# Second attention with one folded query-key product, the normalised image as its keys, and gamma and beta moved into the group norm

## The reference, cut to what matters

```python
def _L1_conv_ref(inputs, gn_gamma, gn_beta, wq, bq, wk, bk, wv, bv, wo, bo):
    GROUPS = 32
    xg = inputs.astype(jnp.float32).reshape(B, H, W, GROUPS, C // GROUPS)
    mean = jnp.mean(xg, axis=(1, 2, 4), keepdims=True)
    var = jnp.var(xg, axis=(1, 2, 4), keepdims=True)
    xg = (xg - mean) * jax.lax.rsqrt(var + EPS)
    x = xg.reshape(B, H, W, C) * gn_gamma + gn_beta
    q = jnp.einsum('bhwc,cd->bhwd', x, wq) + bq
    k = jnp.einsum('bhwc,cd->bhwd', x, wk) + bk
    v = jnp.einsum('bhwc,cd->bhwd', x, wv) + bv
    q = q.reshape(B, N, C) * (1.0 / jnp.sqrt(jnp.float32(C)))
    scores = jnp.einsum('bnc,bmc->bnm', q, k.reshape(B, N, C))
    attn = jax.nn.softmax(scores.astype(jnp.float32), axis=-1)
    out = jnp.einsum('bmc,bnm->bnc', v, attn)
    out = jnp.einsum('bhwc,cd->bhwd', out, wo) + bo
    return out + inputs
```

## Time and profile before

| | |
|---|---|
| median of 3 runs | 79.7 us |
| the runs | 115.36, 79.70, 79.41 us |
| the profiled execution | 79.27 us, of which its span is 77.4 us |
| TensorE busy | 70.6 us (91% of the span) |
| VectorE busy | 51.7 us (67%) |
| ScalarE busy | 33.9 us (44%) |
| GpSimd busy | 24.3 us (31%) |
| granted TensorE clock | 1.0 of full speed |

### The profile page before, as it was taken

One profiled execution on the slowest core, in us unless ns is written; L12 is line 12 of the kernel. 1 busy time (PEld: TensorE's weight loads), 2 busy tenths in 40 slices (PEclk: granted clock), 3 DMA queues, 4 the chain that ended last, 5 costly groups with the idle time before them and its releaser, 6 DMA issues.

```text
span 77.4 us, 1968 instructions
## 1 busy us (share of the span) xinstructions
PE 70.6 (91%) x732; PEld 53.6 (69%) x732; DVE 51.7 (67%) x172; ACT 33.9 (44%) x84; POOL 24.3 (31%) x37
## 2 busy tenths in 40 slices
PE   4999699998999999999999999998897999998950
PEld 2345599783786647879777989845485869996830
DVE  0478742116366959477789968599799786868480
ACT  6112397068139563524424419820248048263600
POOL 5008999900000038390019137123820030000000
PEclk9999999999999999999999999999999999999999
DMA  0789870000000000000000000000000000010112
GB/s 9 226 270 150 305 289 12 0 8 0 0 8 0 0 0 4 0 0 8 0 0 0 4 0 0 8 0 0 0 0 0 0 0 4 0 68 9 59 55 89
DMA packets 3051, 3.07 MB, mean 40 GB/s; under 512 B 225, under 2 KB 2657, under 8 KB 3042
## 3 DMA queue, kind: packets, MB, share of 16 engines
q1 hardware_dynamic: 3042, 2.95, 12.8%
HBM read 2.42 MB, written 0.52 MB: 38 GB/s over the span
## 4 chain that ended last, share of the span: by engine, by line
PE 63%; DVE 17%; issue 5%; DMA 5%; ACT 3%; SPq 2%; POOL 2%; DVEq 0%; POOLq 0%; ACTq 0%
PE bank L810 53%; DMA x_hw<-x 5%; PE bank L971 5%; PE bank L1140 2%; DVE smax L604 2%; DVE x_t L656 1%; DVE gst L694 1%; SPq L247 1%; DVE st L528 1%; DVE bilin L578 1%; DVE x_gn L716 1%; DVE dist_y L562 1%; PE bank L989 1%; DVE q_conv L517 1%; POOL grs L330 1%
## 5 line engine op out<-in xcount | busy, mean ns | idle before, releaser
L810 PE MATMUL bank<-k_blk,qh 128*128 128x512 f32 x16 | 8.4, 605 | 0.0
L810 PE MATMUL bank<-v_blk,p_t 128*128 128x34 f32 x64 | 7.8, 267 | 0.0
L810 PEld LDWEIGHTS bank<-v_blk,p_t 128*128 128x128 f32 x64 | 7.8, 192 | 0.0
L810 PE MATMUL bank<-warm 128*128 128x512 bf16 x18 | 6.3, 471 | 1.0 <-POOL warm L269 1.0
L604 DVE TENSOR_REDUCE smax<-bank 128x8 f32<-128x512 f32 x8 | 5.5, 685 | 2.4 <-PE bank L810 2.4
L317 POOL TENSOR_TENSOR zrs<-zve,neg_half 128x2 f32<-128x2 f32 x4 | 2.9, 714 | 12.7 <-DVE zve L646 12.7
L810 PE MATMUL bank<-q_ph,wd 128*32 128x112 f32 (+5 forms) x256 | 6.8, 249 | 0.0
L303 POOL TENSOR_TENSOR x_res<-x_st,msa_bias 128x1024 f32<-128x1024 f32 x1 | 2.4, 2358 | 12.8 <-DVE bilin L578 12.8
L431 ACT ACTIVATE p_t<-bank 128x512 f32<-128x512 f32 x8 | 4.8, 597 | 3.4 <-PE bank L971 3.4
L810 PEld LDWEIGHTS bank<-q_ph,wd 128*32 128x32 f32 x256 | 5.6, 109 | 0.7 <-issue 0.3
L611 DVE TENSOR_TENSOR s_sub<-bank,smax 128x512 f32<-128x512 f32 x8 | 5.5, 682 | 0.1
(11 more groups left out here) (149 smaller groups left out, 161.2 us busy)
## 6 DMA issues: line engine op xcount, KB each, us to landing
x_st<-x SPq DMA_DIRECT2D x1, 512.0 KB, 6.7
pack_late<-late SPq DMA_DIRECT2D x1, 448.0 KB, 7.3
out<-y SPq DMA_DIRECT2D x3, 128.0 KB, 1.7
pack_fold<-fold SPq DMA_DIRECT2D x1, 320.0 KB, 4.1
pack_mid<-mid SPq DMA_DIRECT2D x1, 261.0 KB, 5.8
x_hw<-x SPq DMA_DIRECT2D x2, 128.0 KB, 2.2
x_hw<-x SPq DMA_DIRECT2D x1, 256.0 KB, 3.8
pack_early<-early SPq DMA_DIRECT2D x1, 184.0 KB, 2.5
```

The lines of the kernel that those rows point to most:

```text
L810: return pe.matmul(o, l, r_, start=start, stop=stop, **k)
```

## The change

It replaces the two projections of the second attention by one. With A = wq wk^T, the part of the scores that depends on both positions is x A x^T. So the query side is x A plus a column (wk times bq), and the key side is the normalised image itself: `k1` and its product and copy are gone. The term that the key bias adds to a whole row, x wq bk, comes out of the value product: `w_vo` gets two more columns, one with wq bk and one with bq bk, both scaled. The row term is then brought into the shift of the exponential in two steps on VectorE, `shift_image`. The values are 130 columns wide now, with the ones in front. Gamma and beta go into the norm: `gn_affine` makes a scale and a shift per channel and image, and GpSimd's three products with gamma are gone, as is the product that carried beta through `w_vo`.

```diff
             z_scale(0)
-            pool.tensor_scalar(wq1g[:, :], w("wq1"), w("gn_gamma"), None, ALU.mult)
-            pool.tensor_scalar(wk1g[:, :], w("wk1"), w("gn_gamma"), None, ALU.mult)
-            pool.wait_ge(s["w_vo_ok"], 1)
-            pool.tensor_scalar(w_vog[:, :], w_vo[:, :], w("gn_gamma"), None, ALU.mult).then_inc(s["gamma_ok"], 1)
...
                 act.wait_ge(s["fold1_mm"], 1)
-                act.copy(w_vo[:, :], bank[7][:, 0:C]).then_inc(s["w_vo_ok"], 1)
-                for j, name in enumerate(("bq1", "bk1", "mlp_b")):
-                    act.activation(cols1[:, j:j + 1], bank[7][:, C + j:C + j + 1], ACT.Identity, bias=w(name)).then_inc(s["cols1_ok"], 1)
+                act.copy(w_vo[:, 0:C], bank[7][:, 0:C])
+                act.activation(w_vo[:, C:C + 2], bank[7][:, C:C + 2], ACT.Copy, scale=C ** -0.5).then_inc(s["w_vo_ok"], 1)
+                act.copy(cols1[:, 0:1], bank[7][:, C + 2:C + 3]).then_inc(s["cols1_ok"], 1)
+                act.activation(cols1[:, 1:2], bank[7][:, C + 3:C + 4], ACT.Identity, bias=w("mlp_b")).then_inc(s["cols1_ok"], 1)
+                act.copy(a1[:, :], bank[7][:, 2 * C:3 * C]).then_inc(s["a1_ok"], 1)
...
-            def norm_image(b):
-                n = b // 2
+            def gn_affine(n):
+
+                i = slice(GN_SETS[n].start, GN_SETS[n].stop)
                 dve.wait_ge(s["gmean_ok"], n + 1)
                 dve.wait_ge(s["grs_ok"], n + 1)
-                dve.tensor_scalar(x_gn[:, b], x1_t[:, b], gmean[:, b:b + 1], grs[:, b:b + 1],
-                                  ALU.subtract, ALU.mult).then_inc(s["xgn_ok"], 1)
+                dve.tensor_scalar(gscale[:, i], grs[:, i], w("gn_gamma"), None, ALU.mult).then_inc(s["gscale_ok"], 1)
+                dve.wait_ge(s["gscale_ok"], n + 1)
+                for b in GN_SETS[n]:
+                    dve.scalar_tensor_tensor(out=gshift[:, b:b + 1], in0=gmean[:, b:b + 1], scalar=gscale[:, b:b + 1], in1=w("gn_beta"),
+                                             op0=ALU.mult, op1=ALU.subtract).then_inc(s["gshift_ok"], 1)
+
+            def norm_image(b):
+                dve.wait_ge(s["gshift_ok"], b + 1)
+                dve.tensor_scalar(x_gn[:, b], x1_t[:, b], gscale[:, b:b + 1], gshift[:, b:b + 1],
+                                  ALU.mult, ALU.subtract).then_inc(s["xgn_ok"], 1)
...
                 dve.tensor_scalar(q1[:, b], bank[3 + b % 2][:, 0:HW], cols1[:, 0:1], C ** -0.5, ALU.add, ALU.mult).then_inc(s["q1_ok"], 1)
-                dve.tensor_scalar(k1[:, b], bank[3 + b % 2][:, HW:2 * HW], cols1[:, 1:2], None, ALU.add).then_inc(s["k1_ok"], 1)
...
+            def shift_image(b):
+
+                t = slice(2 * b, 2 * b + 2)
+                row_term = v1[:, b, :, C + 2]
+                dve.wait_ge(s["nmax1_ok"], b + 1)
+                dve.wait_ge(s["v1_ok"], b + 1)
+                dve.scalar_tensor_tensor(out=ntop1[:, t], in0=nmax1[:, t], scalar=w_vo[:, C + 1:C + 2], in1=row_term,
+                                         op0=ALU.subtract, op1=ALU.subtract).then_inc(s["ntop1_ok"], 1)
+                dve.wait_ge(s["ntop1_ok"], b + 1)
+                dve.scalar_tensor_tensor(out=shift1[:, t], in0=ntop1[:, t], scalar=w_vo[:, C + 1:C + 2], in1=row_term,
+                                         op0=ALU.add, op1=ALU.add).then_inc(s["shift1_ok"], 1)
...
                 mm(bank[7][:, 0:C], w("wv1T"), w("wo1"))
-                mm(bank[7][:, C:C + 1], w("wq1"), w("gn_beta"))
-                mm(bank[7][:, C + 1:C + 2], w("wk1"), w("gn_beta"))
-                mm(bank[7][:, C + 2:C + 3], w("mlp_w"), w("ln_b")).then_inc(s["fold1_mm"], 1)
+                mm(bank[7][:, C:C + 1], w("wq1T"), w("bk1"))
+                mm(bank[7][:, C + 1:C + 2], w("bq1").to_broadcast([P, P]), w("bk1"))
+                mm(bank[7][:, C + 2:C + 3], w("wk1T"), w("bq1"))
+                mm(bank[7][:, C + 3:C + 4], w("mlp_w"), w("ln_b"))
+                mm(bank[7][:, 2 * C:3 * C], w("wq1T"), w("wk1T")).then_inc(s["fold1_mm"], 1)
...
-                mm(bank[3 + b % 2][:, 0:HW], wq1g[:, :], x_gn[:, b])
-                mm(bank[3 + b % 2][:, HW:2 * HW], wk1g[:, :], x_gn[:, b]).then_inc(s["qk_mm"], 1)
+                mm(bank[3 + b % 2][:, 0:HW], a1[:, :], x_gn[:, b]).then_inc(s["q1_mm"], 1)
...
                 for t in range(S):
-                    m = mm(bank[1][:, t * C:(t + 1) * C], x_gn[:, b, t * P:(t + 1) * P], w_vog[:, :])
+                    m = mm(bank[1][:, t * (C + 2):(t + 1) * (C + 2)], x_gn[:, b, t * P:(t + 1) * P], w_vo[:, :])
...
-                    m = mm(bank[5 + b % 2][:, t * HW:(t + 1) * HW], q1[:, b, t * P:(t + 1) * P], k1[:, b])
+                    m = mm(bank[5 + b % 2][:, t * HW:(t + 1) * HW], q1[:, b, t * P:(t + 1) * P], x_gn[:, b])
...
             mm(bank[7][:, 0:C], w("bv1").to_broadcast([P, P]), w("wo1"), stop=False)
-            mm(bank[7][:, 0:C], w("gn_beta").to_broadcast([P, P]), w_vo[:, :], start=False, stop=False)
             mm(bank[7][:, 0:C], ones_row[:, :], r("bo1"), start=False).then_inc(s["outbias_mm"], 1)
```

More of the change, by code:

```diff
@@ L52 @@
     "mid": [("mo_w", C), ("head_of", NH), ("ones_mask", 2), ("grid_x", G * PIX), ("grid_y", S * G * PIX)],
-    "late": [("mlp_w", C), ("wv1T", C), ("wo1", C), ("wq1", C), ("wk1", C), ("group_mean", P), ("group_rest", P)],
+    "late": [("mlp_w", C), ("wv1T", C), ("wo1", C), ("wq1T", C), ("wk1T", C), ("group_mean", P), ("group_rest", P)],
 }
@@ L114, in build @@
         m_kv = sb("m_kv", [P, 2 * C])
-        w_vo = sb("w_vo", [P, C])
+        w_vo = sb("w_vo", [P, C + 2])
+        a1 = sb("a1", [P, C])
         cols = sb("cols", [P, 3])
[L117 to L120, removed]
+        cols1 = sb("cols1", [P, 2])
         mlp_wg = sb("mlp_wg", [P, C])
@@ L164, in build @@
         grs = sb("grs", [P, B])
+        gscale = sb("gscale", [P, B])
+        gshift = sb("gshift", [P, B])
         x_gn = sb("x_gn", [P, B, HW])
         q1 = sb("q1", [P, B, HW])
-        k1 = sb("k1", [P, B, HW])
-        v1 = sb("v1", [P, B, S, C + 1])
+        v1 = sb("v1", [P, B, S, C + 4])
         nmax1 = sb("nmax1", [P, T])
+        ntop1 = sb("ntop1", [P, T])
+        shift1 = sb("shift1", [P, T])
         p1 = sb("p1", [P, 2, S, HW])
@@ L187, in build @@
             "norm of z and MLP": "zst_ok zmv_ok zve_ok zrs_ok zhat_ok zt_mm zt_ok mlp_mm gel_ok zres_ok x1t_ok gelt_mm x1res_ok",
-            "group norm": "gst_ok gmv_ok dev_mm dev2_ok gvar_mm gve_ok gmean_ok grs_ok xgn_ok",
-            "second attention": """qk_mm q1_ok k1_ok v1_mm v1_ok s1_mm nmax1_ok p1_ok p1t0_mm p1t1_mm p1t0_ok p1t1_ok
+            "group norm": "gst_ok gmv_ok dev_mm dev2_ok gvar_mm gve_ok gmean_ok grs_ok gscale_ok gshift_ok xgn_ok",
+            "second attention": """q1_mm q1_ok v1_mm v1_ok s1_mm nmax1_ok ntop1_ok shift1_ok p1_ok p1t0_mm p1t1_mm p1t0_ok p1t1_ok
                 av1_mm rec1_ok y_ok y_out""",
@@ L479, in value_copy @@
                 act.wait_ge(s["v1_mm"], b + 1)
-                act.copy(v1[:, b, :, 0:C], bank[1][:, 0:HW].rearrange("p (s c) -> p s c", s=S)).then_inc(s["v1_ok"], 1)
+                act.copy(v1[:, b, :, 2:C + 4], bank[1][:, 0:S * (C + 2)].rearrange("p (s c) -> p s c", s=S)).then_inc(s["v1_ok"], 1)
             def exp_image(b):
-                act.wait_ge(s["nmax1_ok"], b + 1)
+                act.wait_ge(s["shift1_ok"], b + 1)
                 if b >= 2:
@@ L735, in finish_tile @@
                 dve.wait_ge(s["av1_mm"], i + 1 if b >= 2 else 2 * b + 2)
-                dve.reciprocal(rec1[:, i:i + 1], av_bank(b, t)[:, t * HW + C:t * HW + C + 1]).then_inc(s["rec1_ok"], 1)
+                dve.reciprocal(rec1[:, i:i + 1], av_bank(b, t)[:, t * HW:t * HW + 1]).then_inc(s["rec1_ok"], 1)
                 dve.wait_ge(s["rec1_ok"], i + 1)
-                dve.scalar_tensor_tensor(out=y[:, i], in0=av_bank(b, t)[:, t * HW:t * HW + C], scalar=rec1[:, i:i + 1], in1=x1_res[:, i],
+                dve.scalar_tensor_tensor(out=y[:, i], in0=av_bank(b, t)[:, t * HW + 2:t * HW + C + 2], scalar=rec1[:, i:i + 1], in1=x1_res[:, i],
                                          op0=ALU.mult, op1=ALU.add).then_inc(s["y_ok"], 1)
@@ L774, in _ @@
             zhat_image(3)
+            gn_affine(0)
             norm_image(0)
@@ L791, in _ @@
             max_image(0)
+            shift_image(0)
+            gn_affine(1)
             norm_image(2)
@@ L794, in _ @@
             max_image(1)
+            shift_image(1)
             project_out(2)
@@ L797, in _ @@
             max_image(2)
+            shift_image(2)
             project_out(3)
@@ L800, in _ @@
             max_image(3)
+            shift_image(3)
             probs_out(dve.tensor_copy, dve, 2, 1)
@@ L1163, in value_rows @@
                 for j in range(S):
-                    m = mm(av_bank(b, t)[:, t * HW:t * HW + C + 1], p1_t[:, b % 2, t, j], v1[:, b, j], start=(j == 0), stop=(j == S - 1))
+                    m = mm(av_bank(b, t)[:, t * HW:t * HW + C + 2], p1_t[:, b % 2, t, j], v1[:, b, j, 0:C + 2], start=(j == 0), stop=(j == S - 1))
```

(1 more changed line is left out.)

36 lines of the change are left out of this document (18 added, 18 removed).

## The result

The changed kernel takes 80.26 us in the median of 20 runs (79.76 to 80.87), the kernel before 79.34 us in the median of its 20 (78.89 to 115.36). The ratio is 1.0114, with a 95% interval of 1.0093 to 1.0136: slower by 0.9 us. The ratios leave out single runs that stand clearly above the others of their kernel, as the 115.36 us does. The profiled executions say the same: 80.10 us with a span of 78.2, against 79.27 with a span of 77.4. So 0.83 us of difference can be followed through the traces.

What follows compares the result with a forecast made beforehand. It took the chain through TensorE, with a VectorE stretch from 56 to 60 us, as the bound: 79.27 - 0.88 - 0.39 + 0.42 + 0.42 + 0.50 + 0.20 = 79.54 us, stated as a 79.7 us median, range 78.7 to 80.8.

Steps and rivals of the forecast that it cites:

- VectorE the bound: Seven small VectorE operations delay image 2's `q` from 0.23 us each; at 0.3 us each, +1.0 us, 80.7 us; chance 0.20.
- The step that failed: TensorE's rounds of images 2 and 3: products follow without a gap, so removing the key product gains 2 x 0.44 = 0.88 us.
- The shift: Two small VectorE operations before the exponential: 0.42 us each for images 0 and 3, hidden for images 1 and 2.
- The norm: Scale and shift operations before `x_gn`: +0.5 us for the first pair, beside GpSimd's `z_res`; hidden for the second pair.
- near 0: Other end for the first pair's norm: by bare durations, +0.55 us less what GpSimd's company already costs there.
- The key copy: VectorE's copy of `k`: 0.39 us gained once, for image 0; nothing for the other images.
- The folding: Three places on TensorE's chain, with products of one and of 128 columns added and one of 128 removed: +0.20 us in sum.
- The rest: GpSimd's three removed products gain nothing; two extra columns in the value products cost under 0.05 us in all.
- The first norm is covered: Small operations run while `x_gn` would have waited anyway: term 0 to -0.2 instead of +0.5, 79.2 to 79.0 us; chance 0.22.
- The product's gain stays whole: TensorE finds other work during image 0's wait; both shift costs and the folding hide, first norm covered: 78.0 us; chance 0.04.
- what would show it: Trace signs: TensorE rounds 3.1 instead of 3.5 us, wait for `p` about 0.8 us, `gscale` and `gshift` stretched beside `z_res`.
- One sign of being wrong: Listed signs: `q` of image 2 late, small operations far from 0.21 us, or the stretch before 50 us changed by over 0.2.

Runs made afterwards that it cites:

- the early additions: GpSimd's output-bias additions for images 2 and 3 moved ahead of its last two powers: kernel before 78.73 us (ratio 0.9891), changed kernel 79.31 us (0.9994).

## Why the prediction was right or wrong

It said no change that can be told, within 2% with 0.91, and a sum of +0.27 us over the profiled execution. The kernel became slower by 0.9 us (1.1%), and the interval of the ratio lies wholly above 1. So "within 2%" was right and "no change that this measurement can tell" was not. The range of 78.7 to 80.8 holds the 80.26, but the time lies above the forecast's own 79.3 to 80.1 (0.50), where "VectorE the bound" stood (0.20). Of the +0.84 us in the traces the sum had +0.27.

**The step that failed** is "They follow without a gap, so a product taken out of it is time gained, as long as VectorE and ScalarE keep up", and with it "2 x 0.44 = 0.88 us gained". The gain is 0.50 us, and it is so in all six traces of kernels without the key product whose order on TensorE was left alone: the first to the third transposes take 7.21 us in the kernel before (7.22 with the early additions), and 6.70 to 6.72 in every one of them. The two products between transposes and their use were not only work, they covered ScalarE's copy of the transposes. With both, 0.87 us of products stood there; with one, 0.44 are too few. The condition was named, "as long as VectorE and ScalarE keep up", but not worked out for this copy: I checked the exponential's path against the round and not the copy's. This step is 0.38 of the 0.57 us by which the sum was short.

**The shift** was sized 0.42 at each end, and is 0.51 and 0.37. The place was right, images 0 and 3, and hidden in between. Each of the two steps takes 0.22 us and 0.25 to the next start, the reciprocal that I took as the nearest row 0.17 and 0.21. At the end, 0.14 us were free: before, the transposes of the last image came 0.63 us behind the start of the exponential (71.60 to 72.23), since TensorE was still at the product ahead of them; now they come 0.52 us behind it (72.57 to 73.09), as soon as it is done. That is 0.11 of the 0.14; the rest isn't named. The second figure is the less certain: without the shift this stretch took 4.42 and 4.41 us in two traces and 4.31 or 4.32 in three others, and between the early additions with the shift and without it (4.79 and 4.32) the step is 0.47. So the last shift costs 0.37 to 0.48.

**The norm** was sized +0.5 and is 0.59, with a reason that is half wrong. That small operations with SBUF tiles wait for GpSimd is shown (0.60 and 0.77 us, against 0.22 and 0.35). The exclusive lock on the shared port pair, of which the Trainium skill tells (SBUF — State Buffer, section "SBUF: two separate sides"), agrees with that, for the stretched operations end 0.02 us behind the two `z_res`. But the old norm paid as much (0.72 us), so it cancels, and what is left is the bare time. The "near 0" that I took as the other end, 0.55 less what is lost now, couldn't be reached: the old loss was not a space that other work could fill.

**The key copy** (0.39) came out to the hundredth. **The folding** was sized 0.20 and is 0.26, the same in all seven traces of kernels with it (15.48 or 15.49 us, against 15.22 in the kernel before, with and without the early additions, and 15.21 with the key product out). No run takes the folding out alone. The traces place it: from the transpose before the first fold to the next group of products it is 1.88 us instead of 1.39 (34.57 to 36.45, 34.58 to 35.97), and where the product with beta is gone, 0.64 instead of 0.86. **The rest** at nothing holds: GpSimd's removed products and ScalarE's added copy show nowhere, and the queries of image 2 are 0.41 us early for the scores.

**The rivals.** "VectorE becomes the bound" gave a time near the one measured (80.7 us), but for another reason: small operations cost 0.25 us, over its deciding point of 0.23, and yet `q` wasn't late, since TensorE itself came later to the scores. So the time near its 80.7 is luck for that rival. "The first norm is covered" didn't happen, nor did "The product's gain stays whole". Of "what would show it", the wait of TensorE for `p` (0.92, I said 0.8) and the stretched small operations came; the rounds of 3.1 us didn't, and that one line points at the cause at once. One sign of being wrong came as well: the stretch before 50 us changed by 0.26 us, over the 0.2 named.

## What to carry to other kernels

Before taking an operation out of a full queue, look at what stands behind it: if the next one needs a result that another engine is making meanwhile, the removed work was its cover, and only the part beyond that latency is gained. Before adding a step, ask whether the result needs it: what the shift adds and takes away cancels. A small step isn't small on the chain: the two steps of the shift, on two elements per partition each, cost 0.88 us at the two places where they stood open; the removed products and copy gave 0.89. When a term rests on a stall that exists already, ask whether the old kernel pays it too.

## What the runs showed of the hardware that I had not expected

A VectorE operation on 128x2 elements, with a tile and a column in SBUF, took 0.60 us when GpSimd's addition of 128x256 ran beside it, and 0.22 to 0.23 without: it ended 0.02 us behind the addition, though it moves two elements per partition. Moving two GpSimd additions by two places in its queue, into its idle time, was worth 0.87 us to the kernel before and 0.95 us to the changed one (0.73 and 0.79 in the traces), about as much as the whole change cost.
